# Mixture of a perceiver layer: four tiles by products, an early split, two weight loads ahead of the row loads

## The reference, cut to what matters

```python
x = x + cross_attention(layernorm(x), ctx_1024, mask)     # 4 x 128 tokens, 4 x 2048 keys, width 512
x = x + self_attention(layernorm(x))
# the mixture, on xf = layernorm(x), 512 rows of width C = 512; E = 8 experts, F = 1024, K = 2
logits = normalise(xf, ln_gamma, ln_beta) @ gate_w.T
rw, sel = top_k(softmax(logits), K)
comb = sum(one_hot(sel, E) * rw[..., None], axis=1)
h = gelu(einsum('nc,efc->enf', xf, w1))
y = einsum('enf,ecf->enc', h, w2)
x = x + einsum('enc,ne->nc', y, comb)
```

## Time and profile before

| | us |
|---|---|
| median of 3 runs | 940.02 (939.01 to 942.43) |
| the profiled execution | 939.31 |
| its span | 937.3 |
| first matmul of up(0) | 747.4 |
| first matmul of up(14) | 909.5 |

### The profile page before, as it was taken

The page is one execution under the profiler, slowest core; times in us unless marked ns, Lnnn a source line. Parts: engine busy times, 40 slices in busy tenths (PEclk is TensorE's granted clock), DMA queues, the critical chain, the costliest instruction groups (busy, mean ns, idle before and its releaser), DMA issues. The chain is left out here.

```text
span 937.3 us, 24793 instructions
## 1 busy us (share of the span) xinstructions
PE 877.8 (94%) x10509; PEld 624.9 (67%) x10509; DVE 679.5 (72%) x1022; ACT 528.1 (56%) x811; POOL 389.4 (42%) x294
## 2 busy tenths in 40 slices
PE   5999999999999999999999999989888899999995
PEld 2565777776776776776867766756556786666662
DVE  7956787656788655788657556666778677899982
ACT  3634445565355564355564555443656387899892
POOL 1131775455676345576445545536320052111112
PEclk9999999999999999999999999999989999999998
DMA  9464122442121351221342211308324449999992
GB/s 340 122 179 106 27 66 60 141 118 80 36 70 47 114 150 29 53 63 42 108 114 66 69 46 33 85 11 325 140 90 175 147 143 376 404 400 400 402 337 34
DMA packets 48454, 134.67 MB, mean 144 GB/s; under 512 B 9893, under 2 KB 11813, under 8 KB 44493
## 3 DMA queue, kind: packets, MB, share of 16 engines
q1 hardware_dynamic: 45354, 126.81, 40.0%
q0 software_dynamic: 2800, 6.04, 3.2%
q10 hardware_dynamic: 192, 0.26, 0.1%
HBM read 95.03 MB, written 11.31 MB: 113 GB/s over the span
## 5 line engine op out<-in xcount | busy, mean ns | idle before, releaser
L472 POOL TENSOR_TENSOR acc_pool<-acc_pool,pT 128x1024 f32<-128x1024 f32 x90 | 212.2, 2358 | 144.6 <-ACT pT L744 143.1
L744 ACT ACTIVATE pT<-ps_s 128x1024 f32<-128x1024 f32 x124 | 127.0, 1024 | 195.0 <-PE ps_s L930 194.9
L578 DVE TENSOR_REDUCE mpart<-ps_b 128x1 f32<-128x512 f32 x256 | 173.4, 685 | 70.6 <-PE ps_b L910 69.7
L894 PE MATMUL ps_a<-wv_hi,cT_hi 128*128 128x128 f16 x1024 | 183.5, 219 | 0.0
L896 PE MATMUL ps_a<-wv_hi,cT_lo 128*128 128x128 f16 x1024 | 182.7, 219 | 0.0
L895 PE MATMUL ps_a<-wv_lo,cT_hi 128*128 128x128 f16 x1024 | 182.5, 219 | 0.0
L573 DVE TENSOR_TENSOR k_lo<-k_f,k_hi 128x512 f16<-128x512 f32 x64 | 76.5, 1195 | 58.0 <-ACT k_hi L717 58.0
L894 PEld LDWEIGHTS ps_a<-wv_hi,cT_hi 128*128 128x128 f16 x1024 | 99.8, 97 | 7.9 <-issue 5.9
L895 PEld LDWEIGHTS ps_a<-wv_lo,cT_hi 128*128 128x128 f16 x1024 | 100.2, 98 | 7.2
L896 PEld LDWEIGHTS ps_a<-wv_hi,cT_lo 128*128 128x128 f16 x1024 | 99.8, 97 | 0.0
L910 PE MATMUL ps_b<-k_stack,q_stack 101*128 101x512 f16 x256 | 96.8, 381 | 0.9 <-DVE mpart L578 0.9
(11 more groups left out here) (290 smaller groups left out, 1855.2 us busy)
## 6 DMA issues: line engine op xcount, KB each, us to landing
w_raw<-in_w SPq DMA_DIRECT2D x30, 2048.0 KB, 16.7
raw<-in_context SPq DMA_DIRECT2D x16, 1024.0 KB, 6.1
k_stack<-k_hi SPq DMA_DIRECT2D x252, 64.0 KB, 2.0
k_stack<-k_lo SPq DMA_DIRECT2D x128, 64.0 KB, 2.0
slots_in<-a_zeros SPq DMA_DIRECT2D x1, 3855.0 KB, 13.7
rows_in<-slots_in SPq DMA_DIRECT2D x15, 257.0 KB, 16.5
q_stack<-k_stack SPq DMA_DIRECT2D x12, 128.0 KB, 2.3
x_sb<-in_x SPq DMA_DIRECT2D x2, 512.0 KB, 4.4
```

Of the source, the lines that this page charges most:

```text
L472: nc.gpsimd.tensor_tensor(acc_pool[:, :], pT[:, 0, :] if p == 1 else acc_pool[:, :], pT[:, p % PT, :], ALU.add).then_inc(pool_add, 1)
L578: nc.vector.tensor_reduce(mpart[:, j, kb:kb + 1], bank_at(step)[:, :], AX.X, ALU.max).then_inc(p1_max, 1)
L744: nc.scalar.activation(pT[:, p % PT, :], scores(w, p)[:, :], ACT.Exp, scale=SM_SCALE).then_inc(exp_done, 1)
L894: nc.tensor.matmul(to, cT_hi[:, c, keys], t.wv_hi[:, c, col], start=(c == 0), stop=False)
```

## The change

`EARLY` and `ROWS_AHEAD` go from 3 to 4: tile 3's rows are picked by products too, in the middle of up(2), and SP loads rows four tiles ahead, tiles 0 to 3 before its register reads. SP gets w2_load(3) and w1_load(4), with their waits for w2_low(1) and w1_low(2), ahead of its wait on the scatters. w2_high(1) moves on ACT from the end of k = 1 to the place after the copies of the router's rows, ahead of x_high(0). w2_low(1) moves on DVE from the end of k = 1: its first half ahead of the loop, its second after h_lo(0, 0) and x_low(1).

```diff
-ROWS_AHEAD = 3
+ROWS_AHEAD = 4
-EARLY = 3
+EARLY = 4
@@ SP
+            w2_load(3)
+            w1_load(4)
             sp.wait_ge(sent, 16 * 2 * NB)
             for k in (*range(EARLY, ROWS_AHEAD), *range(EARLY)):
                 rows_load(k)
@@
                 if k + ROWS_AHEAD < TILES:
                     rows_load(k + ROWS_AHEAD)
-                if 4 <= k + 3 < TILES:
+                if 5 <= k + 3 < TILES:
                     w1_load(k + 3)
-                if 3 <= k + 2 < TILES:
+                if 4 <= k + 2 < TILES:
                     w2_load(k + 2)
@@ DVE
-            def w2_low(k):
-                for i in range(PARTS):
+            def w2_low(k, parts=range(PARTS)):
+                for i in parts:
@@
+            w2_low(1, (0,))
             for k in range(TILES):
@@
                     if i == (0 if k + 1 < EARLY else 1) and k + 1 < TILES:
                         x_low(k + 1)
+                    if (k, i) == (0, 0):
+                        w2_low(1, (1,))
                 if k + 2 < EARLY:
                     pick_rows(k + 2)
-                if k:
+                if k >= 2:
                     w2_low(k)
@@ ACT
             for b in range(1, NB):
                 second_copy(b)
+            w2_high(1)
             x_high(0)
@@
-                if k:
+                if k >= 2:
                     w2_high(k)
```

## The result

The changed kernel is slower: 950.84 us (median of 20 runs, 937.12 to 958.03) against 937.36 us of the kernel before on the same chips; the ratio 1.0103 (95% interval 1.0077 to 1.013) counts only the ten of its runs that lie within 1.5% of its fastest, and the ratio of the two medians over all runs is 1.0144. The profiled execution took 950.18 us with a span of 948.4. The forecast was 933.5, a gain of 6.5. The granted clock does not make the difference: from 790 to 870 us it is 1.00 in both profiles.

The account below looks back on a forecast made before the run. The prediction took DMA as the bound, 11.73 us a tile against PE's 11.14. Gaps given back 7.4, less 0.2 and 0.7, made 6.5 us: 940.02 - 6.5 = 933.5 us, range 931.8 to 938.0 (own range 932 to 935.3).

Parts of the forecast that it names:

- The bound: Mixture in steady state: DMA sets the pace at 11.73 us a tile, 0.6 us above PE's own work of 11.14.
- a tile's time before it matters: ROWS_AHEAD 4 makes row load 8 wait for the first add one tile earlier; adds land in 10.9 us, so no cost.
- The 7.4 us: PE's waits before up products, 6.0 marked issue plus 1.4 for low rows, could be given back by earlier DMA.
- rival 1: Mixture: DMA stays the bound to the end if w1(6) lands at 803.4; only 3.5 us gained, 937.0; chance 0.15.
- rival 2: Scatters on POOL: each waits out a whole VectorE pass it meets, 2.2 us more, 935.7 in all; chance 0.13.
- Rival 3: Start of mixture: scatters and row load 0 starve behind w2(3) and w1(4); slower, 953.3 us; chance 0.07.
- Term (b): Start of mixture: y_evict(0) needs row load 0 after the scatters, landing at 775.1, 0.8 us too late; charged 0.7 us.
- Term (a): Mixture from up(4) on: DMA stays ahead of PE, w1(6) landing at 799.5 against 799.9 needed; no cost, hardly any slack.
- Tile 3 by products: Middle of up(2): 32 added matmuls replace four transposes and their wait for rows; PE loses 0.2 us.

Follow-up runs that it names:

- c1: Changed kernel with w2_load(3) and w1_load(4) behind SP's first four row loads, not ahead of the wait on the scatters; ratio 1.0162 to the kernel before.
- f3: Changed kernel with ROWS_AHEAD back at 3, so each row load needs the add of one tile earlier; ratio 1.0124 to the kernel before.
- f4: Changed kernel with SP's loop order turned round, the tile's two weight loads ahead of its row load; ratio 1.0143 to the kernel before.
- f1: Changed kernel with one more VectorE pass per tile, one SBUF input, between w2_low(k) and w1_low(k + 1) from k = 2 on; ratio 1.0118 to the kernel before.
- a4: Changed kernel with the second half of each w1_low cut from 2048 to 1024 columns, VectorE 1.1 us shorter per tile; ratio 1.0002 to the kernel before.
- b2: Changed kernel with the mixture's w1_low and w2_low passes replaced by one-input maximum passes of about the same length; ratio 0.9951 to the kernel before.
- v1: Changed kernel with w2_low(1)'s first half before x_low(0), its second at its old place, and the two early loads behind four row loads; ratio 0.9949.
- e_changed_again: The changed kernel run once more, unaltered; ratio 1.0154 to the kernel before.
- a1: The kernel before with only EARLY and ROWS_AHEAD raised from 3 to 4; ratio 1.0008 to the kernel before.
- a2: Changed kernel with EARLY and ROWS_AHEAD at 3 and without the two early loads, leaving only the early split of w2(1); ratio 1.0055 to the kernel before.
- a3: Changed kernel with EARLY and ROWS_AHEAD at 3, keeping the early split and the two early loads; ratio 1.0069 to the kernel before.
- d1: Kernel before with one more 128x512 VectorE pass per tile, two SBUF inputs, ahead of w2_low(k) from k = 3 on; ratio 0.9977 to the kernel before.
- d2: Kernel before with the same extra pass as d1 but with one SBUF input; ratio 0.9979 to the kernel before.
- v2: v1 with EARLY and ROWS_AHEAD back at 3; ratio 1.0047 to the kernel before.
- v3: v1 with the loop order of f4; ratio 0.9957 to the kernel before.
- b1: Changed kernel with half of each of the mixture's own weight loads (w1 from tile 4, w2 from tile 3) left out; ratio 0.9901 to the kernel before.

## Why the prediction was wrong

The time from the second add's issue to the last one's, out of the POOL timelines, sorts the kernels:

| kernel | second add | last add | between | longest stay on POOL |
|---|---|---|---|---|
| before | 788.12 | 931.29 | 143.2 | 3.5 |
| changed | 789.33 | 942.50 | 153.2 | 10.4 |
| c1 | 790.52 | 944.21 | 153.7 | 11.3 |
| f3 | 787.04 | 940.41 | 153.4 | 11.1 |
| f4 | 789.01 | 943.91 | 154.9 | 10.7 |
| f1 | 790.40 | 940.37 | 150.0 | 6.6 |
| a4 | 791.22 | 928.49 | 137.3 | 2.5 |
| b2 | 787.23 | 925.40 | 138.2 | 2.4 |
| v1 | 782.83 | 925.02 | 142.2 | 3.9 |

The others fit: 154.1 in e_changed_again, 140.7 to 142.9 in a1, a2, a3, d1, d2, v2 and v3, whose longest stays are 2.8 to 3.9, and 134.0 in b1, with half the loads.

Changed against before: 10.0 us in the chain, 1.2 in its start, together 11.2; the spans differ by 11.1.

- **The bound.** I took DMA at 11.73 us a tile for the only thing above PE's 11.14. The step that failed is the half sentence on the adds, "a tile's time before it matters": it put their chain at nothing, and it measured +10.0 us. At 0.72 + 11.0 = 11.7 us a tile the chain had no room left. It stood in the waits of POOL of the kernel before, which I did not read:

```profile
POOL out L1645 <- DMA out<-x_sb,rows_in: 105.7, 11, 11.1
```

  Eleven of fifteen adds waited for the add before. a3 and v2 bear it out: PE lost one wait of 10 us there, no stay was above 3.61, and still the adds ended last.
- **The 7.4 us** of gaps did not come in full where the adds were well, either. In b2, without trouble at the port, the gain is 4.6 us (2.5 to 6.8). There the adds are not the reason, since no add is in its chain that ended last. PE's waits are (from 735 us on):

```profile
PE ps_h L1962 <- issue: 5.0, 8, 1.1
```

  1.7 of them, and 0.66 before a down product, come from the late start, and 3.1 from five up products from 846 on, which wait for weights as in the kernel before. So DMA takes the pace back half way, as in rival 1.
- **What a faster PE triggers.** VectorE's round is now 10.6 us (w2_low at 803.82 and 814.43) and an add takes 11.7 or more, so an add's turn comes later in VectorE's program than that of the one before, until it falls into the 8.9 us of w2_low and w1_low, where it stands for up to 10 us and lands after 21. In the changed kernel one step was enough: the add of 789.33 took 14.72 us, and the next came 1.7 us after the start of x_low (803.22). That the stay costs time is shown by b2 and a4; that the shift of the phase is what brings it there is argued from the timelines (d1 holds its phase, b1 stands 5 us in five tiles running), not tried by itself. After the two long adds the next four landed in 12.6 to 14.0 instead of 11.0; SP then issues both weight loads in the same moment as the add. That these loads slow it is argued only.
- **The port rule.** I had it as rival 2 and priced it at the scatters alone, 2.2 us. The same rule at the adds is the loss. My argument against it, that a scatter had taken 1.90 us under the same passes, was no argument: stays run from 1.5 to 11.3 us by where the turn falls.
- **Rival 3** had the right sign with the wrong mechanism. Scatters and row load 0 were late by a few us, not starved.
- **Term (b), the late start**, was right in kind and small in size: scatters complete at 774.5, not 771.1 (POOL +3.5 where I took 2.4, landing 9.8 where I took 7.5), y_evict(0) at 777.3, not 775.1, and PE's waits 2.3 us, not 0.7.
- **Term (a)** held only in part: no up product waited for DMA from 794 to 870, but in b2, whose loads SP issued on time, they did from 846 on. w2_high(1) at 738.45 to 742.1, hidden as forecast; w2_low(1) at 749.46 and 752.87, hidden for VectorE, x_low(1) at 752.27, but not for POOL: that was its price. w1_load(4) left at 762.36 (762.3). The period of PE was 10.98, below the forecast 11.14. The last down product waited 2.54, as before.
- **Tile 3 by products** was forecast at +0.2 us of PE and measured at nothing alone (a1); that it is worth 1% beside early loads (v1 against v2) was not seen.

## What to carry to other kernels

Before giving idle time back to the busiest engine, list every serial chain with its time per round, the slow outputs too: here three of them (DMA, PE, the adds) lay within 0.6 us, and the one that was not in the chain that ended last took over. Give an indirect DMA from GpSimd a place in VectorE's program where no pass with two SBUF inputs runs; a kernel paced by something else may give it that place by luck of phase, and a faster one take it away. Put weight loads behind small transfers that others wait for: two early loads cost the scatters 7 us.

## What the runs showed of the hardware

An indirect DMA's instruction on POOL took 0.97 us (scatter) or 1.54 us (add) at its shortest, and no more beside 128x2048 passes with one SBUF input (1.54 at 809.19 in b2). It took 9.3 to 11.3 us when its turn fell within the first 2.3 us of four successive 128x2048 passes with two SBUF inputs, which two shorter such passes follow. All twenty stays above 4 us, in seven profiles, ended 1.5 us after the start of a pass with one SBUF input. Stays of 2.6 to 3.7 us show that an instruction also gets in between two passes with two inputs (789.33 in the changed kernel); when it does is open. VectorE's passes were not longer during the long stays (4.47 to 4.50 us a pair). Eight scatters of 128 rows had landed 2.8 to 4.2 us after the last was issued with no weight load in flight (c1, v1), and 9.8 to 15.2 us with early weight loads on their way (changed, b2).
